# Reciprocal roots of four layer norms on GpSimd, projection biases as weight rows, residual copies by DMA

## The chip, the cores and the metric

One core of one Trainium2 chip runs the whole program. The metric is the device time of one execution in microseconds (us). Engines are named as in the profile: PE (TensorE matmul), PEld (its weight loads), DVE (VectorE), ACT (ScalarE), POOL (GpSimd), SP (SyncE, which here issues transfers).

## The reference, cut to what matters

Sixteen images with their texts give 324 tokens of 192 channels each. Two transformer layers follow. The change touches the first layer (L0) and the shared-key attention of the second (L1), above all the layer norms, the two projection biases and the residual sums.

```python
def _layernorm(x, axis=-1, eps=1e-05):
    m = jnp.mean(x, axis=axis, keepdims=True)
    v = jnp.var(x, axis=axis, keepdims=True)
    return (x - m) / jnp.sqrt(v + eps)
...
h = _L0_tok_ref(x, L0_tok_W)
h = jnp.concatenate([h, txt], axis=1)
h = h + _L0_attn_ref(_layernorm(h), ..., L0_attn_W_proj, L0_attn_b_proj)      # ends in  out @ W_proj + b_proj
h = h + _L0_ffn_ref(_layernorm(h), ...)
h = h + _L1_attn_ref(_layernorm(h), ..., L1_attn_W_proj, L1_attn_b_proj)      # softmax attention, out @ W_proj + b_proj
h = h + _L1_ffn_ref(_layernorm(h), ...)                                       # a second norm of its own, router, attention, MLP
```

## The kernel before

Tokens lie on partitions: 324 tokens are three tiles of 108 partitions (P = 108, T = 3), 192 channels in the free dimension. The program has two stages. The first goes through the 16 batches and does everything up to the spill of the routed inputs; the second stage does the last feed-forward block. Between them two passes weave both.

A pass of the first stage works on several batches at once. The string ORDER_1 lists its steps, and every engine walks the same list in the same order, doing its own share of each step. OFF_1 says by how many batches a step runs ahead. In the string `s` is one score matmul with its exponential, `a` the weighted sum of values, `m` one block of scores whose row maximum DVE takes (`mxh`), `r` the transposes that bring the maxima (`mp`) to rows. The named steps are those of the layers: `ln1` to `ln4` the norms, `t1` to `t5` transposes of normed tokens, `tok` the patch embedding, `qk`, `v`, `val`, `hid`, `out`, `proj`, `proj4` products. Each engine works strictly in this order, so a step that waits holds back every step behind it on its engine.

Each norm is cut in steps: step 0 takes statistics (`bn_stats`, tile `st`), step 1 aggregates them to mean and variance (tile `mv`) and starts a Newton iteration for the reciprocal root (a first guess from the bits in tile `rs`, then three rounds of three small DVE instructions, tile `nt`), step 2 does two of the rounds, step 3 subtracts the mean and multiplies (`normalised`, tiles `xn`, for ln4 `xna` and `xn5`). For ln4 the root of a second norm directly behind it comes out of the same variances. Each of these small instructions waits for the one before it (`link`). Ring buffers in PSUM (`lin` with two banks for products, `mps` with three for the maxima) tie DVE and ACT to PE: PE may fill a bank only when its reader has emptied it.

The residual sums read an addend from SBUF: `hb` is the token tile plus the bias of the first projection, `hab` is `hc` plus the bias of the second, and `hc` is a copy of `h` from one pass to the next. POOL makes all three (steps `hb`, `hab`, `hc`), besides bf16 pieces of q and k (`parts`, tile `piece`) and `hx`. POOL also issues the fetch of the next tokens (`xload`). SP issues the other transfers in the order of the list: the pieces to DRAM (`todram`, scr_q and scr_k), from there packed into `qpack` and `kpack` (`pack0` to `pack2`), the softmax denominators out and their reciprocals back (`den`, `spread`, tile `bc`).

Of the kernel before, what the change touches and what calls it, by code (L numbers as in the profile page):

```python
# [30 lines left out]
EPS4, EPS5 = 1e-5, 1e-6  # L31
# [231 lines left out]
def build(nc, A):  # L263
# [3 lines left out]
    with ctx:  # L267
# [16 lines left out]
        b_p0 = sb("b_p0", [P, C])  # L284
# [5 lines left out]
        b_p1 = sb("b_p1", [P, C])  # L290
# [19 lines left out]
        hb = sb("hb", [P, T, C])  # L310
# [5 lines left out]
        mv = sb("mv", [P, T, 2])  # L316
        var = sb("var", [P, 2 * T])
        rs = sb("rs", [P, 2 * T])
        nt = sb("nt", [P, 2 * T])
# [195 lines left out]
        ln4_done = signal("ln4_done", 2)  # L515
        nmz_ready = signal("nmz_ready")
# [24 lines left out]
        MEMSETS_POOL, SETUP_POOL, SETUP_DVE = 10, 14, 10  # L541
# [9 lines left out]
        NFIRST, NLOAD = len(FIRST) + 1, len(LOADS) + 7  # L551
# [8 lines left out]
        def _(sp):  # L560
# [4 lines left out]
            sp.dma_start(b_p0[:, :], A["b_p0"].partition_broadcast(P)).then_inc(loads_first.sem, 16)  # L565
# [9 lines left out]
            sp.dma_start(b_p1[:, :], A["b_p1"].partition_broadcast(P)).then_inc(loads.sem, 16)  # L575
# [45 lines left out]
            def denominators(att, name, k, j):  # L621
# [13 lines left out]
                else:  # L635
# [79 lines left out]
        def _(pool):  # L715
# [6 lines left out]
            for n, (x, value) in enumerate(((of[64:KP, :, :, :], 0.0), (xS[KC:KP, :, :], 0.0), (v1[:, :, :, :], 0.0),  # L722
# [3 lines left out]
                                            (bc[:, :, :], 1.0))):  # L726
# [35 lines left out]

            def first_step(name, k, c, what, j, i):
                if name == "shared":
                    shared_pieces()
                    both_layers()
                elif name == "xload":
# [3 lines left out]
                    pool.wait_ge(hb_ready.sem, hb_ready.at(j - 1, 1))  # L771
# [6 lines left out]
                elif name == "hab":  # L778

                    front.emptied(pool, i, "proj4_1")  # L780
                    pool.wait_ge(hc_ready.sem, hc_ready.at(j, 1))
                    for t in range(T):
                        done = nc.gpsimd.tensor_tensor(hab[:, t, :], hc[:, t, :], b_p1[:, :], ALU.add)
                    done.then_inc(hab_ready.sem, 1)
                elif name == "hc":

                    front.emptied(pool, i, "out_1")
                    pool.wait_ge(hab_ready.sem, hab_ready.at(j - 1, 1))
                    pool.sem_inc(gate_pool.sem)
                    nc.gpsimd.tensor_copy(hc[:, :, :], h[:, :, :]).then_inc(hc_ready.sem, 1)  # L790
                elif name == "hb":

# [842 lines left out]
```

## Time and profile before

| | |
|---|---|
| median of 3 runs | 2161.02 us (2160.82 to 2162.99) |
| the profiled execution's own time | 2163.17 us |
| its span, first to last instruction | 2161.4 us |
| PE busy | 1898.0 us, 88% |
| DVE busy | 1425.0 us, 66% |
| ACT busy | 1119.6 us, 52% |
| POOL busy | 267.0 us, 12% |
| mean granted TensorE clock | 0.962 |

The rows further down come from the profiled execution, so their sums are held against 2161.4 us of span. A row of a timeline has the start in us, the length, engine, line, operation and tiles, how many instructions it merges, and in brackets how long the engine was idle before it and for whom. One pass of the first stage takes about 82 us. PE busy time counts a matmul until its modelled end, so PE counts as idle only when nothing at all is under way on it.

### The profile page before, as it was taken

What the parts mean: (1) busy time and instruction counts of PE and PEld (TensorE: products, weight loads), DVE (VectorE), ACT (ScalarE), POOL (GpSimd) and SP (SyncE); (2) the same over time, 40 slices, a digit from 0 to 9 for tenths busy, and PEclk for the clock granted to TensorE, in tenths of its full rate; (3) what the DMA queues carried; (4) which work ended last, traced back from release to release, by engine and by line L of the source; (5) the groups of instructions that cost most, each with busy time, mean ns of one, the idle gap of its engine ahead of it and who ended that gap; (6) DMA issues with size and microseconds to landing.
All of it is one profiled execution on the core that took longest, in us unless ns stands there. A gap on an engine that the chain in (4) does not pass through costs nothing. (4 is left out here: it accounts for less than half of the span.)

```text
span 2161.4 us, 42850 instructions
## 1 busy us (share of the span) xinstructions
PE 1898.0 (88%) x11904; PEld 1267.3 (59%) x11904; DVE 1425.0 (66%) x4566; ACT 1119.6 (52%) x2585; POOL 267.0 (12%) x406
## 2 busy tenths in 40 slices
PE   3688998998998998998998987767899999999996
PEld 2465665666665666665665654434566666666664
DVE  3267777767867867868868866524677656566563
ACT  1244554554554554554554554353565656566563
POOL 4301101101101101101101101100011001001000
PEclk9799999999999999999999999978999999999998
DMA  4202112112112112112122021302334333433431
GB/s 150 53 16 55 49 32 61 37 39 60 42 39 56 40 45 57 40 47 57 37 51 57 27 55 51 80 25 68 76 89 114 78 97 94 110 93 89 115 83 35
DMA packets 157452, 134.86 MB, mean 62 GB/s; under 512 B 31924, under 2 KB 136344, under 8 KB 157208
## 3 DMA queue, kind: packets, MB, share of 16 engines
q1 hardware_dynamic: 153592, 127.90, 22.7%
q0 software_dynamic: 2304, 4.79, 0.9%
q8 instruction: 58, 0.95, 0.2%
q10 hardware_dynamic: 1440, 0.75, 0.1%
q14 instruction: 58, 0.48, 0.1%
HBM read 81.96 MB, written 50.16 MB: 61 GB/s over the span
## 5 line engine op out<-in xcount | busy, mean ns | idle before, releaser
L1228 DVE TENSOR_REDUCE mxh<-mps 108x1 f32<-108x260 f32 (+1 forms) x1728 | 684.5, 442 | 351.2 <-PE mps L1400 340.3
L943 ACT ACTIVATE prob<-sps 108x324 f32<-108x324 f32 x1536 | 623.1, 439 | 523.5 <-PE sps L1370 477.6
L1400 PE MATMUL mps<-kpack,qpack 96*108 96x260 bf16 (+1 forms) x1728 | 420.9, 298 | 56.2 <-DMA kpack<-scr_k 25.0
L1370 PE MATMUL sps<-qpack,kpack 128*108 128x324 bf16 x1536 | 440.8, 321 | 33.4 <-ACT prob L943 26.7
L1400 PEld LDWEIGHTS mps<-kpack,qpack 96*108 96x108 bf16 x1728 | 220.5, 131 | 210.4 <-DVE mxh L1228 86.7
L1385 PE MATMUL aps<-prob,v 128*32 128x324 f32 x3072 | 318.5, 459 | 3.7 <-ACT prob L943 1.2
L1370 PEld LDWEIGHTS sps<-qpack,kpack 128*108 128x108 bf16 x1536 | 192.2, 129 | 211.8 <-ACT prob L943 149.9
L1356 PE MATMUL lin<-yT,w 128*128 128x324 f32 x576 | 186.0, 455 | 18.1 <-ACT g L843 13.7
L1356 PEld LDWEIGHTS lin<-yT,w 128*128 128x128 f32 x576 | 103.6, 194 | 63.8 <-issue 32.7
L1385 PEld LDWEIGHTS aps<-prob,v 128*32 128x32 f32 x3072 | 73.2, 110 | 105.2 <-issue 60.3
L758 POOL CAST piece<-rest 128x324 bf16<-128x324 f32 x96 | 43.6, 454 | 729.5 <-DVE rest L1060 721.9
L777 POOL TENSOR_TENSOR hx<-ha,xna 108x576 f32<-108x576 f32 x16 | 22.4, 1397 | 863.2 <-DVE xna L1030 863.2
L1356 PE MATMUL lin<-xT,w_in 128*128 128x324 f32 x384 | 119.8, 445 | 0.5 <-ACT xT L839 0.5
L1346 PE MATMUL lin<-w,g 128*108 128x192 f32 x576 | 108.0, 329 | 2.7 <-PEq L136 2.7
L1346 PE MATMUL lin<-w_out,g 128*108 128x192 f32 x576 | 108.1, 330 | 2.0 <-PEq L136 2.0
L1329 PE MATMUL lin<-ident,xn 108*96 108x108 f32 x384 | 62.2, 284 | 46.3 <-DVE xn L1030 37.5
L957 ACT COPY av<-aps 128x324 f32<-128x324 f32 x96 | 41.1, 428 | 103.2 <-PE aps L1385 78.0
L1346 PEld LDWEIGHTS lin<-w,g 128*108 128x108 f32 x576 | 91.2, 173 | 5.7 <-issue 3.4
L1346 PEld LDWEIGHTS lin<-w_out,g 128*108 128x108 f32 x576 | 92.0, 176 | 4.2 <-issue 2.5
L943 ACT ACT_TABLE_LOAD x65 | 83.4, 1283 | 14.8 <-PE sps L1370 12.9
L843 ACT ACT_TABLE_LOAD x66 | 84.7, 1283 | 8.7 <-PE lin L1356 7.6
L1356 PEld LDWEIGHTS lin<-xT,w_in 128*128 128x128 f32 x384 | 68.0, 193 | 28.2 <-ACT g L843 5.1
(157 smaller groups left out, 2402.4 us busy)
## 6 DMA issues: line engine op xcount, KB each, us to landing
qpack<-scr_q SPq DMA_DIRECT2D x96, 243.0 KB, 3.3
kpack<-scr_k SPq DMA_DIRECT2D x96, 121.5 KB, 3.3
scr_q<-piece SPq DMA_DIRECT2D x32, 243.0 KB, 3.1
scr_k<-piece SPq DMA_DIRECT2D x32, 243.0 KB, 4.0
kpack<-scr_k SPq DMA_DIRECT2D x96, 81.0 KB, 3.1
bc<-rec_d SPq DMA_DIRECT2D x128, 60.8 KB, 2.4
scr_q<-piece SPq DMA_DIRECT2D x32, 162.0 KB, 3.5
scr_q<-piece SPq DMA_DIRECT2D x64, 81.0 KB, 3.4
```

Source lines behind the costliest of these rows:

```text
L758: nc.gpsimd.tensor_copy(piece[:, m, 1, :], rest[:, m, :]).then_inc(att.second.sem, 1)
L777: nc.gpsimd.tensor_tensor(hx[:, :, :], ha[:, :, :], xna[:, :, :], ALU.add).then_inc(hx_ready.sem, 1)
L843: nc.scalar.activation(g[:, f, :], ring.at(i, what)[:, 0:N], ACT.Gelu, bias=b_in[:, f:f + 1] if bias else 0.0).then_inc(ring.free["act"].s ...
L943: nc.scalar.activation(prob[0:rows, n % NP, :], sps[0:rows, n % 2, 0:N], ACT.Exp, scale=SCALE).then_inc(att.exped.sem, 1)
L957: nc.scalar.copy(av[:, q, :], aps[:, 0:N]).then_inc(att.copied.sem, 1)
L1228: nc.vector.tensor_reduce(mxh[:, hd, t, s:s + 1], att.mps.at(i, use)[0:P, 0:att.width], AX.X, ALU.max, negate=True).then_inc(att.mps.free[ ...
L1329: done = nc.tensor.transpose(b[0:KC, t * P:(t + 1) * P], src[:, t, k * KC:(k + 1) * KC], ident[0:P, 0:P])
L1346: done = mm(tiles2(b)[0:P, t % 2, :], acts[k][:, t * P:(t + 1) * P], weights[k], start=k == 0, stop=k == 5)
L1356: done = mm(b[0:size, 0:N], w[:, k, c:c + size], x[:, k, 0:N], start=k == 0, stop=k == 1)
L1370: mm(sps[0:rows, n % 2, 0:N], kpack[:, 4 * q + n % 4, k * att.rows:k * att.rows + rows], qpack[:, 4 * q + n % 4, :], start=True, stop=True ...
L1385: mm(aps[32 * hd:32 * hd + 32, 0:N], att.values[:, k, 4 * q + hd, :], prob[:, n % NP, :], start=k == 0, stop=k == kt - 1).then_inc(att.sum ...
L1400: mm(bank[0:P, 0:att.width], qpack[0:6 * D, 4 * q + hd, t * P:(t + 1) * P], kpack[0:6 * D, 4 * q + hd, s * att.width:(s + 1) * att.width], ...
```

## The change

Four things are changed.

- The Newton iterations leave DVE. DVE's step 1 of a norm is now only the aggregation (into `mean`, one tile for each norm), which signals POOL. POOL adds the epsilon (`vars4`; for ln4 a second instruction makes the variance of the second norm) and raises the result to the power -0.5 with one `tensor_tensor`, operation pow, against a tile of -0.5. DVE's step 3 (for ln4 its step 2 and 3) waits for POOL's `root`. Step 2 of ln1 to ln3 is gone, and `hx` is listed behind ln4_2.
- Both projection biases become a row of the weights. For the first, row 96 of `aT` is set to one and row 96 of `w_p0` holds the bias. For the second the softmax denominator row of head 0 is multiplied by its own reciprocal and so is one; for this one of the four `bc` transfers writes 32 partitions where it wrote 16. The matmuls keep their number and shape.
- `hc` and `hab` become transfers that SP issues, 108x576 each. `hb` is gone: the residual of `proj` reads the token tile `hin` itself.
- The next tokens are fetched behind `proj_1`, at the end of a pass; it stood behind `dft_0.0`, some three slots of the list earlier.

```diff
 ORDER_1 = (
-    "a ln2_1 m m m s v_0.0 s ln2_2 ln2_3 s s m v_0.1 m s m p v_1.0 s recip s",
+    "a ln2_1 m m m s v_0.0 s ln2_3 s s m v_0.1 m s m p v_1.0 s recip s",
...
-    "hid5 m m s s m proj4_0.0 m den m proj4_0.1 s spread0 spread1 proj4_1 s s ln4_0 a s hx ln4_1 r ln4_2 s",
+    "hid5 m m s s m proj4_0.0 m den m proj4_0.1 s spread0 spread1 proj4_1 s s ln4_0 a s ln4_1 r ln4_2 hx s",
...
-    "s m s ln3_0 tok.0 s tok.1 m m m s hab t4_0 t4_1 ln3_1 s m hb m a m log m s t5_0",
-    "exp p m ln3_2 s s ln3_3 t5_1 s m m s a",
+    "s m s ln3_0 tok.0 s tok.1 m m m s hab t4_0 t4_1 ln3_1 s m m a m log m s t5_0",
+    "exp p m s s ln3_3 t5_1 s m m s a",
...
-    "a s t1_0 t1_1 s s ln1_2 ln1_3 zv s",
-    "val_0.0 zs val_0.1 s val_1 pack0 zt s m m m dft_0.0 m m xload p pack1 m a m s m m dft_0.1 m s m m dft_1.0 m m",
+    "a s t1_0 t1_1 s s ln1_3 zv s",
+    "val_0.0 zs val_0.1 s val_1 pack0 zt s m m m dft_0.0 m m p pack1 m a m s m m dft_0.1 m s m m dft_1.0 m m",
...
-    "inv_0.1 inv_1.0 inv_1.1 s r proj_0.0 proj_0.1 proj_1 s ln2_0 a",
+    "inv_0.1 inv_1.0 inv_1.1 s r proj_0.0 proj_0.1 proj_1 xload s ln2_0 a",
...
                     for hd in range(4):
-                        sp.dma_start(bc[32 * hd:32 * hd + D, :, :], rec_d[hd].partition_broadcast(D)).then_inc(att.bc_in.sem, 16)
+                        n = 32 if hd == 0 and att is one else D
+                        sp.dma_start(bc[32 * hd:32 * hd + n, :, :], rec_d[hd].partition_broadcast(n)).then_inc(att.bc_in.sem, 16)
...
+                elif name == "hc":
...
+                    sp.dma_start(hc[:, :, :], h[:, :, :]).then_inc(hc_ready.sem, 16)
+                elif name == "hab":
...
+                    sp.dma_start(hab[:, :, :], hc[:, :, :]).then_inc(hab_ready.sem, 16)
...
+            def reciprocal_roots(n, j):
+
+                pool.wait_ge(spread_known[n].sem, spread_known[n].at(j, 1))
+                pool.sem_inc(gate_pool.sem)
+                nc.gpsimd.tensor_scalar(vars4[:, n, 0], mean[n][:, :, 1], EPS4, None, ALU.add).then_inc(vars_known[n].sem, 1)
+                if n == 3:
+                    nc.gpsimd.tensor_scalar(vars4[:, n, 1], mean[n][:, :, 1], 1.0 + EPS5, EPS4 * EPS5, ALU.mult,
+                                            ALU.add).then_inc(vars_known[n].sem, 1)
+                w = 2 if n == 3 else 1
+                pool.wait_ge(vars_known[n].sem, vars_known[n].at(j, w))
+                nc.gpsimd.tensor_tensor(root[n][:, 0:w, :], vars4[:, n, 0:w, :], minus_half[:, 0:w, :],
+                                        ALU.pow).then_inc(root_known[n].sem, 1)
...
                     pool.wait_ge(ln1_done.sem, ln1_done.at(j - 1, 1))
-                    pool.wait_ge(hb_ready.sem, hb_ready.at(j - 1, 1))
+                    front.emptied(pool, i, "proj_1")
...
-            def newton(w, times):
-                for _ in range(times):
-                    link(nc.vector.tensor_tensor(nt[:, 0:w], rs[:, 0:w], rs[:, 0:w], ALU.mult))
-                    link(nc.vector.scalar_tensor_tensor(nt[:, 0:w], nt[:, 0:w], -0.5, var[:, 0:w], ALU.mult, ALU.mult))
-                    link(nc.vector.scalar_tensor_tensor(rs[:, 0:w], nt[:, 0:w], 1.5, rs[:, 0:w], ALU.add, ALU.mult))
-
-            def variances(w):
+            def variances(n):
                 for t in range(T):
...
+                    done = nc.vector.bn_aggr(mean[n][:, t, :], st[:, t, :])
+                done.then_inc(spread_known[n].sem, 1)
...
                 else:
-                    normalised(src, dst, rs).then_inc(signals.sem, 1)
+                    dve.wait_ge(root_known[n].sem, root_known[n].at(j, 1))
+                    normalised(src, dst, n, root[n][:, 0]).then_inc(signals.sem, 1)
...
-                    residual(front, i, what, k, h, hb)
+                    residual(front, i, what, k, h, hin)
...
-        "w_p0": padded(rows(a["L0_attn_W_proj"], KC)),
-        "b_p0": a["L0_attn_b_proj"],
+        "w_p0": with_bias(padded(rows(a["L0_attn_W_proj"], KC)), a["L0_attn_b_proj"], KC, 1),
...
-        "w_p1": by_heads(a["L1_attn_W_proj"]),
-        "b_p1": a["L1_attn_b_proj"],
+        "w_p1": with_bias(by_heads(a["L1_attn_W_proj"]), a["L1_attn_b_proj"], D, 0),
```

The first place is DVE around the second norm: the aggregation (`mv` before, `mean` after), the root, three row maxima (`mxh`), and the normalisation `xn`. Before:

```order
L1017 BN_AGGR mv<-st 108x2 x3
L1019 TENSOR_SCALAR var<-mv 108x3
L1025 TENSOR_SCALAR rs<-var 108x3
L1011 TENSOR_TENSOR nt<-rs 108x3
L1012 SCALAR_TENSOR_TENSOR nt<-nt,var 108x3
L1013 SCALAR_TENSOR_TENSOR rs<-nt,rs 108x3
L1228 TENSOR_REDUCE mxh<-mps 108x1 x3
```

Six more Newton instructions follow there before the normalisation. After the change:

```order
L1034 TENSOR_TENSOR h<-lin,hin 108x384
L1034 TENSOR_TENSOR h<-lin,hin 108x192
L1007 BN_STATS st<-h 108x6 x3
L1003 ISA
L1012 BN_AGGR mean<-st 108x2 x3
L1209 TENSOR_REDUCE mxh<-mps 108x1 x3
L1017 TENSOR_SCALAR xn<-h,mean,root 108x192 x3
```

Between the aggregation and the normalisation only the three maxima are left, and the normalisation waits for POOL's `root`.

The second place is POOL over one pass, from `hx` to the fetch of tokens. Before:

```order
L777 TENSOR_TENSOR hx<-ha,xna 108x576
L783 TENSOR_TENSOR hab<-hc,b_p 108x192 x3
L800 TENSOR_TENSOR hb<-hin,b_p 108x192 x3
L790 COPY hc<-h 108x576
L758 CAST piece<-rest 128x324
L760 TENSOR_TENSOR piece<-rest,piece 128x324
```

After the change, from the fetch of one pass to the first piece of the next:

```order
L725 DMA pT<-in_x 128x392
L726 DMA hin<-in_txt 20x192
L727 DMA hin<-in_txt 108x192
L776 TENSOR_SCALAR vars<-mean 108x3
L782 TENSOR_TENSOR root<-vars,minus_half 108x3
L776 TENSOR_SCALAR vars<-mean 108x3
L778 TENSOR_SCALAR vars<-mean 108x3
L782 TENSOR_TENSOR root<-vars,minus_half 108x6
L802 TENSOR_TENSOR hx<-ha,xna 108x576
L776 TENSOR_SCALAR vars<-mean 108x3
L782 TENSOR_TENSOR root<-vars,minus_half 108x3
L767 CAST piece<-rest 128x324
```

The three issues of the fetch now stand directly ahead of the root of ln2; the wide root is that of ln4, and the last root that of ln3. The root of ln1 comes behind the three pairs of pieces.

## Rows read from the trace of the kernel before

**Rows 1.** First line of the page.

```profile
span 2161.4 us, 42850 instructions
```

**Rows 2.** Windows: us, then busy time of each engine, clock, DMA.

```profile
120.00:1306.00 1186.00, 1073.20 (x6994) 731.28 (x6995) 885.83 (x3059) 624.63 (x1477) 150.05 (x238) 0.98 0.17 45
```

**Rows 3.** Waits of PE from 120 to 1306: total, times, longest.

```profile
PE lin L1329 <- DVE xn L1030: 20.1, 34, 1.1
...
PE mps L1400 <- DMA kpack<-scr_k: 14.8, 13, 1.8
...
PE mps L1400 <- DVE mxh L1228: 10.1, 20, 1.5
```

**Rows 4.** Waits of PE from 1306 to 1480, the woven passes.

```profile
PE mps L1400 <- DVE mxh L1228: 5.0, 4, 2.1
...
PE lin L1337 <- DVE ha L1049: 1.9, 2, 1.5
```

**Rows 5.** Waits of PE from 0 to 120, the start.

```profile
PE lin L1329 <- DVE xn L1030: 16.7, 3, 6.0
```

**Rows 6.** Groups by line on DVE: busy us, mean ns, idle before.

```profile
L1011 DVE TENSOR_TENSOR nt<-rs 108x3 f32<-108x3 f32 (+1 forms) x192 | 43.7, 228 | 6.5 <-DVEq L140 1.7
```

**Rows 7.** Groups by line on POOL.

```profile
L800 POOL TENSOR_TENSOR hb<-hin,b_p 108x192 f32<-108x192 f32 x48 | 27.0, 588 | 67.0 <-issue 30.3 <-ACT hin L882 29.8 <-ACTq L140 6.8
L777 POOL TENSOR_TENSOR hx<-ha,xna 108x576 f32<-108x576 f32 x16 | 22.4, 1397 | 863.2 <-DVE xna L1030 863.2
...
L1625 POOL MEMSET const-float32-1.0<- 128x1 f32 x1 | 0.1, 108 | 0.0
```

**Rows 8.** Timeline of DVE around ln2 of one pass.

```profile
701.36 1.01 DVE L1049 TENSOR_TENSOR h<-lin,hb 108x384 f32<-108x384 f32 x2 [1.72 <-PE lin L1337]
...
703.83 0.31 DVE L1017 BATCH_NORM_AGGREGATE mv<-st 108x2 f32<-108x6 f32 x3 [0.55 <-DVE st L1006]
...
707.47 0.96 DVE L1030 TENSOR_SCALAR xn<-h,mv,rs 108x192 f32<-108x192 f32 x3
```

**Rows 9.** Timeline of PE, its first transposes for ln2.

```profile
708.56 0.48 PE L1329 MATMUL lin<-ident,xn 108*96 108x108 f32 x3 [0.51 <-DVE xn L1030]
```

**Rows 10.** Timeline of DVE around ln3, same pass.

```profile
656.35 0.30 DVE L1017 BATCH_NORM_AGGREGATE mv<-st 108x2 f32<-108x6 f32 x3
...
657.47 0.56 DVE L1011 TENSOR_TENSOR nt<-rs 108x3 f32<-108x3 f32 x1
...
662.21 0.96 DVE L1030 TENSOR_SCALAR xn<-h,mv,rs 108x192 f32<-108x192 f32 x3
```

**Rows 11.** Timeline of DVE around ln1, same pass.

```profile
671.68 0.30 DVE L1017 BATCH_NORM_AGGREGATE mv<-st 108x2 f32<-108x6 f32 x3
...
675.48 0.96 DVE L1030 TENSOR_SCALAR xn<-hin,mv,rs 108x192 f32<-108x192 f32 x3
```

**Rows 12.** Timeline of POOL beside it.

```profile
671.95 0.45 POOL L758 CAST piece<-rest 128x324 bf16<-128x324 f32 x1 [1.22 <-DVE rest L1060]
672.49 0.80 POOL L760 TENSOR_TENSOR piece<-rest,piece 128x324 bf16<-128x324 f32 x1
677.22 0.58 POOL L717 DMA_DIRECT2D pT<-in_x  x1 [3.93 <-PE lin L1329]
```

**Rows 13.** Timeline of PE, its transposes for ln1.

```profile
676.57 0.76 PE L1329 MATMUL lin<-ident,xn 108*96 108x108 f32 x6 [0.75 <-DVE xn L1030]
```

**Rows 14.** Timeline of DVE around ln4, same pass.

```profile
726.89 0.31 DVE L1017 BATCH_NORM_AGGREGATE mv<-st 108x2 f32<-108x6 f32 x3
...
729.53 0.96 DVE L1030 TENSOR_SCALAR xna<-ha,mv,rs 108x192 f32<-108x192 f32 x3
```

**Rows 15.** Waits of SP's queue over one pass, 650 to 732.

```profile
SPq L614 <- ACT prob L943: 20.4, 2, 20.2
```

**Rows 16.** Timeline of SP: issue of the bc transfers.

```profile
711.23 1.69 SPq L641 DMA_DIRECT2D bc<-rec_d  x4
```

**Rows 17.** Timeline of DVE: the multiplication that reads bc.

```profile
719.48 1.16 DVE L1075 TENSOR_TENSOR av<-av,bc 128x972 f32<-128x972 f32 x1
```

More of the change, by code:

```diff
@@ L315, in build @@
         st = sb("st", [P, T, 6])
[L316 to L319, printed above, removed]
+        mean = [sb(f"mean{n}", [P, T, 2]) for n in range(4)]
+        root = [sb(f"root{n}", [P, 2, T]) for n in range(4)]
+        vars4 = sb("vars4", [P, 4, 2, T])
+        minus_half = sb("minus_half", [P, 2, T])
         xT1 = sb("xT1", [KP, 2, N])
@@ L508, in build @@
         x_in = signal("x_in", 48, prime=0)
-        hb_ready = signal("hb_ready")
-        hab_ready = signal("hab_ready")
-        hc_ready = signal("hc_ready")
+        hab_ready = signal("hab_ready", 16)
+        hc_ready = signal("hc_ready", 16)
         ln1_done = signal("ln1_done")
@@ L515, in build @@
         ln4_done = signal("ln4_done", 2)
+        spread_known = [signal(f"ln{n + 1}_spread") for n in range(4)]
+        root_known = [signal(f"ln{n + 1}_root") for n in range(4)]
+        vars_known = [signal(f"ln{n + 1}_vars", 2 if n == 3 else 1) for n in range(4)]
         nmz_ready = signal("nmz_ready")
@@ L721, in _ @@
             load_x(0)
-            for n, (x, value) in enumerate(((of[64:KP, :, :, :], 0.0), (xS[KC:KP, :, :], 0.0), (v1[:, :, :, :], 0.0),
+            for n, (x, value) in enumerate(((of[64:KP, :, :, :], 0.0), (aT[KC:KP, :, :], 0.0), (aT[KC:KC + 1, :, :], 1.0),
+                                            (xS[KC:KP, :, :], 0.0), (v1[:, :, :, :], 0.0),
                                             (kpack[KC:KP, :, :], 0.0), (yA[KC:KP, :, :], 0.0),
@@ L766, in first_step @@
                     both_layers()
+                elif name in ("ln1", "ln2", "ln3", "ln4"):
+                    if k == 1:
+                        reciprocal_roots(number(name) - 1, j)
                 elif name == "xload":
@@ L777, in first_step @@
                     nc.gpsimd.tensor_tensor(hx[:, :, :], ha[:, :, :], xna[:, :, :], ALU.add).then_inc(hx_ready.sem, 1)
[L778 to L791, printed above, removed]
-                    if isinstance(i, int) and i == -2:
-                        pool.wait_ge(loads_first.sem, 16 * NFIRST)
-                    else:
-                        front.emptied(pool, i - 1, "proj_1")
-                    front.emptied(pool, i, "tok")
-                    pool.wait_ge(x_in.sem, x_in.at(j, 48))
-                    for t in range(T):
-                        done = nc.gpsimd.tensor_tensor(hb[:, t, :], hin[:, t, :], b_p0[:, :], ALU.add)
-                    done.then_inc(hb_ready.sem, 1)
                 elif name == "qk":
@@ L976, in _ @@
         def _(dve):
-            for x in (xT1[KC:KP, :, :], aT[KC:KP, :, :], vz[KC:KP, :, :], xT2[KC:KP, :, :], qpack[KC:KP, :, :], cntb[:, :, :],
+            for x in (xT1[KC:KP, :, :], vz[KC:KP, :, :], xT2[KC:KP, :, :], qpack[KC:KP, :, :], cntb[:, :, :],
                       selall[:, :], gateall[:, :], work[:, :]):
@@ L1176, in first_step @@
                     elif k == 1:
[L1177 to L1178 removed]
+                        variances(3)
                     elif k == 2:
[L1180 to L1187 removed]
+                        dve.wait_ge(root_known[3].sem, root_known[3].at(j, 1))
+                        normalised(ha, xna, 3, root[3][:, 0]).then_inc(ln4_done.sem, 1)
+                    else:
+                        dve.wait_ge(root_known[3].sem, root_known[3].at(j, 1))
+                        normalised(ha, xn5, 3, root[3][:, 1]).then_inc(ln4_done.sem, 1)
                 elif name == "log":
@@ L1578, in by_heads, with with_bias @@
         return w.reshape(GROUPS, 128, C).transpose(1, 0, 2)
+    def with_bias(w, b, p, k):
+        w = w.copy()
+        w[p, k] = b
+        return w
     nh = a["x"].shape[2] // 16
```

57 lines of the change are left out of this document (18 added, 39 removed), and 2 rows, old and new, of the table OFF_1.

## The prediction

> **What bounds the kernel now.** I read the windows by stage first, then PE's waits in the same windows, then DVE, POOL, PE and SP in the timeline of one pass. The span is 2161.4 us [rows 1]. In the passes of the first stage PE is busy for 1073.2 of 1186 us, DVE for 885.8 [rows 2]: PE is the bound, with 9.5% of the time in which nothing is under way on it. So work taken off DVE is worth only what PE's idle time before it was worth. In that window PE waited 20.1 us for normed tokens, 10.1 us for a bank of maxima that DVE had not yet read, and 14.8 us for the transfer that fills `kpack` [rows 3]. In the woven passes it waited 5.0 us for the maxima and 1.9 us for a residual sum [rows 4], at the start three times for normed tokens, 16.7 us in all [rows 5]. The reader should see that the named DVE waits which the norms can cause are some 35 us in all after the start, and that the second stage has no norm in it.
>
> **The Newton instructions.** Each norm has eleven of them (epsilon, first guess, nine of three rounds), ln4 fifteen: 48 for a batch, 768 in all. A group of them has a mean of 228 ns [rows 6], so they take about 10 us of DVE in a pass of 82. What that is worth is read norm by norm; take P as the time of one power on POOL.
>
> **The new chain.** Aggregation, hand-over to POOL, addition, power, hand-over to DVE. A hand-over costs 0.13 us: `xn` ends at 707.47 + 0.96 = 708.43 [rows 8] and PE starts at 708.56 [rows 9]. From one POOL instruction to the next that waits for it are 672.49 - (671.95 + 0.45) = 0.09 us [rows 12]. POOL's additions take 588 ns for 192 elements and 1397 ns for 576, so 2.1 ns an element and 0.19 us at three elements; a memset of one element takes 108 ns [rows 7]. The chain is T = 0.13 + 0.19 + 0.09 + P + 0.13 = P + 0.54, and P + 0.73 for ln4 with its second addition.
>
> P has no row. Below it is bounded by an addition, 0.19 us. Above I take a power as a logarithm, a product and an exponential, some 25 steps; if each cost as much as a whole small instruction, that is 25 x 0.19 = 4.8 us. The work is three elements a partition in one instruction, without 25 dispatches, so it is nearer the lower end: I take 1 us, T = 1.54, and keep 0.2 and 4.8 for the range. The Trainium skill, page "GPSIMD Engine Reference", section "Engine selection", says to keep elementwise work on VectorE and that GPSIMD is about twice as slow with two inputs. If that held against the whole Newton string of ln4, the power would cost 4.6 us and the kernel would be slower; no row here shows a power.
>
> **ln2.** The aggregation ends at 704.14, the normalisation starts at 707.47: 3.33 us [rows 8], and PE then waited 0.51 [rows 9]. With three maxima still between, T up to 3.33 - 0.51 = 2.82 removes the whole wait, so P up to 2.3.
>
> **ln3.** From 656.65 to 662.21 are 5.56 us [rows 10]: POOL has room for any P here. Five Newton instructions stood ahead of the maxima, one of them 0.56 us long beside POOL's `hb`, and PE waited for the maxima behind them; `hb`, `hab` and `hc` leave POOL too. The 10.1 us of waits for maxima should go.
>
> **ln1.** POOL is busy with a piece until 673.29 [rows 12], so the root starts there, and `xn` at 673.29 + 1.54 = 674.83 where it was at 675.48 [rows 11]. PE's wait of 0.75 [rows 13] shrinks by 0.65. But this gives nothing in the end: the `kpack` transfer behind it depends on pieces made before ln1 and not on the norm, and PE already waited 14.8 / 13 = 1.1 us for it in a pass [rows 3]. What PE gains ahead, it waits there. The same cover protects: T up to 675.48 - 673.29 + 1.1 = 3.3 us costs nothing.
>
> **ln4.** DVE has no work between aggregation and normalisation, 727.20 to 729.53, 2.33 us [rows 14]. New: 1.73. P above 1.6 makes everything behind it late, one for one.
>
> **The sum.** Normed tokens: 20.1 us less the share of ln1, 14 passes x 0.75 = 10.5, leaves 9.6. Maxima: 10.1. Woven passes: the Newton strings are part of why DVE is late there; I take half of 5.0 + 1.9, 3.4. Start: four norms are waited for openly, and each chain gets shorter by about 2.33 - 1.54 = 0.8, so 3 us. Together 26 us. 2161.4 - 26.1 = 2135.3 us of span; the profiled execution had 1.8 us around its span (2163.17) and stood 2.15 above the median, so 2135 as a median.
>
> **What I cost at nothing.** `hc` and `hab` as transfers: SP issues two more in a pass, some 0.35 us each, and stands 20.4 us in one wait for ACT [rows 15]; they read and write long before their users a pass or half a pass later. Behind `hc` on SP stands the store of pieces; without cover it would be late by 0.35 a pass, 5 us in all. The wider `bc` transfer: issued until 712.92 [rows 16], read at 719.48 [rows 17], 6.5 us of cover. Bias rows: same matmuls; two memsets more on POOL at the start, where its first root may be 0.5 us late. The fetch at the end of the pass has half a pass until `tok`. But its three issues of about 0.58 us [rows 12] now run from 702.4, when the last `h` is summed [rows 8], to about 704.15, and the root of ln2 stands behind them; its aggregation ends at 704.14, so they cost nothing.
>
> **The rivals.**
> *The power is slow, so the kernel is slower.* The place is DVE's new wait in ln4, where nothing else can run, with row maxima queued behind it for which PE waits. It decides from the point at which ln4's loss (P - 1.6) eats the gains of 0.51 at ln2 and about 1 at ln3: at P = 2.7, ln2 keeps 0.1, ln4 loses 1.1. At P = 4 a pass has T = 4.54: ln2 +1.2, ln3 -1.0, ln1 +1.2, ln4 +2.4, so +3.8; 14 passes and 5 us at the start make +58, 2219 us. For it: a power in software has no row, and the string it replaces took only 2.33 us. Against: three elements. Chance 0.15.
> *The fetch delays ln2.* POOL's issues were made while DVE stood idle; now they run beside its statistics. If they took three times as long, 5.2 us, the root would be known at 709.2, 2.2 us past the room; 14 times 2.2 less the 26 gained, and 7 lost at ln2's share: about 2173. Nothing in the rows shows such a stretch. Chance 0.05.
> *The gain is given back.* PE leaves each gap earlier only to find ACT's exponentials or transfers not ready, as at ln1. Then only start and woven passes give anything, 6 us: 2155 to 2160. Chance 0.13, of which 0.08 lies within 0.2%.
> *DVE's lead is worth more than the named waits.* Busy PE hides short stalls in its modelled ends; 10 us less DVE work a pass could shorten those and the 10.5 us of ln1 too: up to 50 us, 2111. Chance 0.12.
> *The forecast*, 2122 to 2150, holds 0.55.
>
> **How the numbers follow.** 2135 is the likeliest case. The range 2108 to 2180 takes in the given-back gain, the stronger gain and the delayed fetch, and leaves out most of the slow power. 0.2% is 4.3 us, about what a measurement of this kernel can tell from no change. Faster by more: 0.55 + 0.12 + 0.05 = 0.72. Same: 0.08. Slower: 0.15 + 0.05 = 0.20.
>
> **What would show it.** In the trace after, POOL's power on 108x3 should be near 1 us, and DVE in ln4 should stand idle for about 1.7 us between aggregation and `xna`. PE's waits for normed tokens in the passes should fall from 20.1 to under 10 us and the wait for maxima to near zero, while that for `kpack` stays or grows by about what ln1 gave. A pass should be 1.4 us shorter. A power over 2.7 us, POOL issues stretched beyond a microsecond, or a `kpack` wait that grows by more than ln1's share would make it wrong.

## The result and the profile after

The kernel after took 2093.71 us (median of 4 runs, 2092.38 to 2097.8), before 2162.01 us (4 runs): ratio 0.9687, 95% interval 0.967 to 0.9704, 68 us faster. The same kernel on two other chips (e9 and e16 below) stood at 0.972 (0.9703 to 0.9738) and 0.9718 (0.97 to 0.9736) of before, 61 us faster. Forecast were a gain of 26 us and a time of 2135 us, with a range from 2108 to 2180. The direction was right, and the size was less than half of what came.

The page after and its groups on POOL (busy, mean ns of one, idle before):

```profile
span 2090.6 us, 42205 instructions
...
PE 1876.9 (90%) x11904; PEld 1262.7 (60%) x11904; DVE 1271.1 (61%) x3797; ACT 1112.2 (53%) x2583; POOL 289.0 (14%) x441
...
L782 POOL TENSOR_TENSOR root<-vars,minus_half 108x3 f32<-108x3 f32 (+1 forms) x64 | 63.9, 999 | 5.3
L776 POOL TENSOR_SCALAR vars<-mean 108x3 f32<-108x3 f32 x64 | 15.4, 241 | 564.3 <-DVE mean L1012 563.6 <-POOL minus_half L738 0.3
```

The price with no row is known now: the power takes 0.88 us on 108x3 and 1.35 us on 108x6, 1.0 in the mean of all (taken: 1 for each), the addition 0.24 (taken: 0.19). DVE lost 154 us of busy time. PE's busy time fell by 21 us too (1898.0 before), though it runs the same 11904 matmuls. That is the first sign of where the rest of the gain lies.

PE's waits after, in the passes (110 to 1242), answer to [rows 3]:

```profile
PE sps L1351 <- ACT prob L944: 22.1, 60, 1.1
...
PE mps L1381 <- DMA kpack<-scr_k: 6.5, 9, 1.0
...
PE mps L1381 <- DVE mxh L1209: 1.4, 6, 0.3
PE lin L1310 <- DVE xn L1017: 0.7, 1, 0.7
```

Normed tokens (20.1) and maxima (10.1) are gone from the list, as forecast, and more fully than forecast, which left up to 10 us for the tokens. The wait for `kpack`, which was to stay, fell from 14.8 to 6.5 in this execution; two later ones of the same kernel have 15.6 and 13.1. The woven passes (1242 to 1413) answer to [rows 4]: nearly nothing changed.

```profile
PE mps L1381 <- DVE mxh L1209: 4.1, 5, 1.6
...
PE lin L1318 <- DVE ha L1034: 2.0, 2, 1.5
```

DVE's new waits in the passes, the first at ln1 and ln2 (at ln3 the root is ready in time), the second at ln4:

```profile
DVE xn L1017 <- POOL root L782: 40.4, 29, 2.5
DVE xna L1017 <- POOL root L782: 30.4, 14, 2.2
```

At ln4 it is 2.17 us a pass, 0.44 more than the 1.73 forecast; 0.35 of it is POOL's power on 108x6, which takes 1.35 us and not 1.

**Where the time came from.** The kernel has sixteen `hx` instructions, one a pass. From the first to the fourteenth are thirteen passes: 81.9 us each before, 77.6 after, 78.2 in e9. The start up to the first `hx` went from 238.3 to 227.3 us (e9: 228.0). From the sixteenth to the end e9 took as long as before, 691.6 us; the first execution took 687.2. Windows of those thirteen passes, before and then e9 (us, busy time of PE, PEld, DVE, ACT, POOL with their instructions, clock, DMA):

```profile
238.30:1302.80 1064.50, 964.79 (x6332) 657.10 (x6331) 805.39 (x2788) 563.08 (x1339) 137.67 (x219) 0.98 0.18 47
```

```profile
228.00:1245.20 1017.20, 940.15 (x6332) 651.29 (x6331) 678.54 (x2164) 557.01 (x1340) 154.12 (x244) 0.99 0.21 56
```

The same 6332 matmuls: the stretch is 47.3 us shorter, PE's idle time fell from 99.7 to 77.1 (by 22.7) and its busy time by 24.6. Half of the gain was never visible as idle time. The granted clock (0.98 and 0.99) does not explain it, since forms of matmul that nobody kept waiting have the same mean. What got shorter are the transposes, which stood behind the stalls (by 4.9 us in all), the matmuls of the maxima (by 3.6) and those of the scores (by 3.3). Groups of PE in these windows, before and then e9:

```profile
L1356 PE MATMUL lin<-xT,w_in 128*128 128x324 f32 x312 | 96.3, 440 | 0.0
L1346 PE MATMUL lin<-w_out,g 128*108 128x192 f32 x469 | 87.3, 326 | 0.0
...
L1329 PE MATMUL lin<-ident,xn 108*96 108x108 f32 x312 | 49.2, 277 | 19.1 <-DVE xn L1030 18.9
```

```profile
L1337 PE MATMUL lin<-xT,w_in 128*128 128x324 f32 x312 | 96.2, 439 | 0.0
L1327 PE MATMUL lin<-w_out,g 128*108 128x192 f32 x469 | 87.3, 325 | 0.0
...
L1310 PE MATMUL lin<-ident,xn 108*96 108x108 f32 x312 | 44.3, 257 | 0.0
```

### The profile page after: what moved, and what is told of

Read it like the earlier page. It is cut to its first block and busy times, and to the rows that moved or that the text cites. A ratio compares the mean times of both kernels' runs of the same rounds, so it can differ in the third digit from the quotient of the medians.

```text
span 2090.6 us, 42205 instructions
## 1 busy us (share of the span) xinstructions
PE 1876.9 (90%) x11904; PEld 1262.7 (60%) x11904; DVE 1271.1 (61%) x3797; ACT 1112.2 (53%) x2583; POOL 289.0 (14%) x441
## 5 line engine op out<-in xcount | busy, mean ns | idle before, releaser
L1381 PE MATMUL mps<-kpack,qpack 96*108 96x260 bf16 (+1 forms) x1728 | 416.0, 296 | 34.3 <-DMA kpack<-scr_k 14.4
L776 POOL TENSOR_SCALAR vars<-mean 108x3 f32<-108x3 f32 x64 | 15.4, 241 | 564.3 <-DVE mean L1012 563.6
L944 ACT ACT_TABLE_LOAD x64 | 82.1, 1283 | 14.8 <-PE sps L1351 13.0
L1045 DVE TENSOR_TENSOR rest<-lin,piece 128x324 f32<-128x324 f32 x96 | 47.2, 492 | 61.9 <-ACT piece L854 28.3
```

The source lines that it names most:

```text
L776: nc.gpsimd.tensor_scalar(vars4[:, n, 0], mean[n][:, :, 1], EPS4, None, ALU.add).then_inc(vars_known[n].sem, 1)
L944: nc.scalar.activation(prob[0:rows, n % NP, :], sps[0:rows, n % 2, 0:N], ACT.Exp, scale=SCALE).then_inc(att.exped.sem, 1)
L1045: nc.vector.tensor_tensor(rest[:, m, :], ring.at(i, what)[:, 0:N], piece[:, m, 0, :], ALU.subtract).then_inc(ring.free["dve"].sem, 1)
L1381: mm(bank[0:P, 0:att.width], qpack[0:6 * D, 4 * q + hd, t * P:(t + 1) * P], kpack[0:6 * D, 4 * q + hd, s * att.width:(s + 1) * att.width], ...
```

## The experiments

Seventeen runs. "Against before" is the ratio with its interval of 95%, "pass" the mean of the thirteen passes in the profiled run in us. The last three columns are PE's waits from 130 to 1230 us: for normed tokens (`xn`), for maxima (`mxh`) and for `kpack`.

| run | against before | pass | xn | mxh | kpack |
|---|---|---|---|---|---|
| before | 1 | 81.9 | 18.1 | 9.5 | 14.1 |
| after | 0.9687 (0.967 to 0.9704) | 77.6 | 0.7 | 1.1 | 6.5 |
| e1 Newton strings back | 0.9827 (0.9804 to 0.985) | 79.8 | 19.2 | 2.0 | 5.3 |
| e2 roots only | 0.9765 (0.9734 to 0.9795) | 78.7 | none | 1.1 | 17.3 |
| e3 fetch late only | 0.9966 (0.9949 to 0.9982) | 81.5 | 11.9 | 10.1 | 2.5 |
| e4 after, fetch early | 0.9769 (0.9744 to 0.9794) | 79.0 | none | 0.8 | 24.8 |
| e5 copies and rows only | 0.9894 (0.9875 to 0.9913) | 80.8 | 19.4 | 1.7 | 14.6 |
| e6 power twice | 0.9819 (0.9793 to 0.9844) | 79.9 | 11.1 | 10.4 | 9.9 |
| e7 copies on POOL | 0.9738 (0.9717 to 0.976) | 78.4 | 0.8 | 0.4 | 9.6 |
| e8 last piece on DVE | 0.9746 (0.9724 to 0.9767) | 78.6 | 0.7 | 0.7 | 17.7 |
| e9 after again | 0.972 (0.9703 to 0.9738) | 78.2 | 0.7 | 0.8 | 15.6 |
| e10 power twice in ln4 | 0.979 (0.9774 to 0.9806) | 79.1 | 0.7 | 10.3 | 12.5 |
| e11 maximum in ln4 | 0.9715 (0.9698 to 0.9731) | 78.0 | 0.7 | 1.1 | 13.0 |
| e12 scores in inv | 0.9749 (0.9735 to 0.9763) | 78.2 | 0.7 | 1.1 | 15.3 |
| e13 store by ACT | 0.9711 (0.9696 to 0.9725) | 77.9 | 0.7 | 1.1 | none |
| e14 e13 and e8 | 0.9713 (0.97 to 0.9727) | 78.1 | 0.7 | 1.1 | 0.2 |
| e15 e13 and e11 | 0.9679 (0.9666 to 0.9692) | 77.9 | 0.7 | 1.1 | none |
| e16 after, third time | 0.9718 (0.97 to 0.9736) | 78.0 | 0.7 | 1.1 | 13.1 |
| e17 e15, beside e16 | 0.969 (0.9674 to 0.9705) | 78.1 | 0.7 | 1.1 | 0.9 |

**e1 to e4: one part undone, or one part alone.** The theory after the first comparison was that the Newton strings were the loss and stalls longer than they look; the rivals were the transfers and POOL's copies.

e1 takes the kernel after and puts the Newton code back:

```diff
+                    newton(T, 2)
...
-                    dve.wait_ge(root_known[n].sem, root_known[n].at(j, 1))
-                    normalised(src, dst, n, root[n][:, 0]).then_inc(signals.sem, 1)
+                    normalised(src, dst, rs).then_inc(signals.sem, 1)
```

> The kernel after, with the Newton strings back on DVE in their old places; the two transfers for the residual copies, the bias rows and the late fetch stay. Theory S (the strings were the loss: each stall of PE behind them was 0.25 to 0.35 us longer than its visible idle time, and this holds at ln1 too): nearly all of the 68 us comes back, 2145 to 2160 us. Theory T (transfers: the late fetch shortens the chain from the pieces to kpack, which is what let the gain at ln1 through): about a third of the gain stays, 2130 to 2145. Theory C (hb, hc and hab left POOL, which sped up DVE beside them): half or more stays, 2120 to 2135.

Measured: 0.9827, 1.07% above e9, 23 us; its 2129 us lie inside Theory C's range. Theory S, which wanted nearly all of the gain back, falls; 37 us of the gain stay without the roots.

e2 is before with `reciprocal_roots` on POOL, with the steps of the list that this changes, and nothing else:

> The kernel before, with only the roots moved to POOL; hb, hc and hab stay POOL's, the biases are added as before, the fetch stays early. Theory S: 2093 to 2108 us, within 15 us of the kernel after. Theory T: ln1's share of some 1.1 us a pass is waited for at kpack again, so 2108 to 2125. Theory C: POOL's copies stand in the way of the roots (a root behind hb or hc waits up to 1.5 us) and slow DVE, 2120 or more. If the parts simply add, this kernel and e1 lie as far from before and after as each other.

Measured: 0.9765, 51 us faster than before. Theory C's obstacle did not show, and PE's wait for normed tokens is gone with a wait for `kpack` of 17.3. What the roots give alone (51) and what remains without them (37) add up to more than the whole: two parts remove the same loss. Where it lies comes with e5.

e3 is before with this alone:

```diff
-    "... dft_0.0 m m xload p pack1 ...
+    "... dft_0.0 m m p pack1 ...
...
-    "inv_0.1 inv_1.0 inv_1.1 s r proj_0.0 proj_0.1 proj_1 s ln2_0 a",
+    "inv_0.1 inv_1.0 inv_1.1 s r proj_0.0 proj_0.1 proj_1 xload s ln2_0 a",
...
+                    front.emptied(pool, i, "proj_1")
                     pool.sem_inc(gate_pool.sem)
```

> The kernel before, with only the fetch of the next tokens moved behind the projection. Theory T: the issue of qpack, which stood behind the stores of pieces, comes some 0.5 us earlier in a pass, PE's wait for kpack falls from 14.8 us to about 8, and the time by 5 to 10 us (2151 to 2157). Theory S: DVE's ln1 is what PE waits for first, so less than 4 us either way (2158 to 2166). If POOL's three issues cost something beside ln2's statistics, it is slower by up to 14 x 0.5 = 7 us.

Measured: 0.9966, 7 us, with the wait for `kpack` down from 14.1 to 2.5 us.

e4 is after with `xload` back behind `dft_0.0` and a step `hb` by which SP copies the tokens, `sp.dma_start(hb[:, :, :], hin[:, :, :])`, since `hin` is overwritten early:

> The kernel after, with the fetch early again, for which the tokens are copied to hb by a transfer in every pass. Theory T: the fetch runs beside the stores of pieces again, kpack comes 0.5 us or more later in each pass and PE waits for it: 7 to 15 us slower than after, 2100 to 2108. Theory S: less than 4 us slower, 2090 to 2098.

Measured: 0.9769; against e9 10.6 us slower, with 24.8 us of waits for `kpack` where e9 has 15.6. It has the added copy in it, so not all of this need be the fetch. Both runs agree with Theory T in sign and size. The medians from issue to landing of the packs, in before and in e3:

```profile
qpack<-scr_q SPq DMA_DIRECT2D x39, 243.0 KB, 3.4
kpack<-scr_k SPq DMA_DIRECT2D x39, 121.5 KB, 3.9
```

```profile
qpack<-scr_q SPq DMA_DIRECT2D x39, 243.0 KB, 3.1
kpack<-scr_k SPq DMA_DIRECT2D x39, 121.5 KB, 3.3
```

In e4 these medians are 3.2 and 3.3 although the fetch is early, so they alone do not carry the reading. The starts in the timelines do: from the issue of a pass's first pack to PE's first matmul on the new `kpack` it took 5.1 us in e4 and 4.6 in e9, means of the thirteen passes.

**e5: the copies and bias rows alone.** e1 with e4's fetch, so Newton on DVE and the fetch early (`hx` is listed behind ln4_2, as in after):

> The kernel before, with hb, hc and hab made by transfers and the biases as weight rows; Newton strings on DVE and the fetch early. e1 and e3 differ in just these copies and stand 1.4% apart. Theory C (POOL's additions slow DVE's Newton instructions beside them: the first guess 259 ns in before, 172 in e1; nt 231 and 200): the strings are as slow or fast whatever the fetch does, so a similar 20 to 30 us, ratio to before 0.986 to 0.991. Theory K (what DVE gains is waited for at kpack as long as the fetch runs ahead of the packs, as in e2 and e4): under 12 us, ratio 0.994 or more, and PE's wait for kpack at 20 us or more.

Measured: 0.9894, 23 us faster, inside Theory C's range. The waits for maxima are gone (1.7 us) with every Newton instruction still there. The timeline of DVE at ln3 shows why. In e5:

```profile
645.43 0.17 DVE L1011 TENSOR_SCALAR var<-mv 108x3 f32<-108x3 f32 x1
645.63 0.17 DVE L1017 TENSOR_SCALAR rs<-var 108x3 int32<-108x3 int32 x1
645.84 0.16 DVE L1003 TENSOR_TENSOR nt<-rs 108x3 f32<-108x3 f32 x1
```

and in before, where POOL makes `hb` from 655.72 to 657.41 and `hc` behind it:

```profile
656.92 0.51 DVE L1025 TENSOR_SCALAR rs<-var 108x3 int32<-108x3 int32 x1
657.47 0.56 DVE L1011 TENSOR_TENSOR nt<-rs 108x3 f32<-108x3 f32 x1
658.06 0.16 DVE L1012 SCALAR_TENSOR_TENSOR nt<-nt,var 108x3 f32<-108x3 f32 x1
...
655.72 1.69 POOL L800 TENSOR_TENSOR hb<-hin,b_p 108x192 f32<-108x192 f32 x3 [3.73 <-ACT hin L882]
657.35 0.66 POOL L790 COPY hc<-h 108x576 f32<-108x576 f32 x1
```

Beside a POOL instruction two of the string took 0.51 and 0.56 us in place of 0.17 and 0.16. Each ended 0.02 us behind POOL's instruction beside it: at 657.43 behind the last addition of `hb` (657.41), at 658.03 behind the copy `hc` (658.01). The Trainium skill, page "Advanced Engine Details and Errata", section "Mode Summary" under "VectorE Performance Modes", says that VectorE's second SBUF port is shared with GpSimd and that GpSimd's instructions and VectorE's two-port ones block each other; the rows agree with a block, though they do not show which port it is. At the end of ln4 the same happens beside `hab`. In before:

```profile
732.10 0.51 DVE L1185 TENSOR_TENSOR nt<-nt,rs 108x3 f32<-108x3 f32 x1
732.65 0.52 DVE L1186 TENSOR_TENSOR nt<-nt,rs 108x3 f32<-108x3 f32 x1
...
732.01 1.68 POOL L783 TENSOR_TENSOR hab<-hc,b_p 108x192 f32<-108x192 f32 x3
```

and in e5:

```profile
720.66 0.16 DVE L1177 TENSOR_TENSOR nt<-nt,rs 108x3 f32<-108x3 f32 x1
720.86 0.16 DVE L1178 TENSOR_TENSOR nt<-nt,rs 108x3 f32<-108x3 f32 x1
```

Over the thirteen passes the small instructions and the second normalisation at these two places are 22 us shorter in e5. This loss goes when the strings leave or when the copies leave. That is the overlap: roots alone 2.35%, copies and rows alone 1.06%, both (e4) 2.31% and not 3.41%, which makes 24 us. It lies in one stretch, and both places lie in it. From `hx` to the last piece of q and k a pass took 24.5 us before, 23.2 in e5, 22.6 in e2 and 22.7 in e4: 1.3 and 1.9 alone but 1.8 together, so 1.4 us a pass and 22 us in sixteen are counted twice.

**e7: after with `hc` and `hab` on POOL.**

```diff
-                    sp.dma_start(hab[:, :, :], hc[:, :, :]).then_inc(hab_ready.sem, 16)
+                    nc.gpsimd.tensor_copy(hab[:, :, :], hc[:, :, :]).then_inc(hab_ready.sem, 1)
```

> The kernel after, with hc and hab as copies by POOL again (no bias in them; each some 0.66 us or more for 576 elements), no transfers. Theory C1 (POOL's copies cost only through the Newton strings, which are gone): within 5 us of after, ratio to before 0.966 to 0.971. Theory C2 (they slow whatever DVE does beside them): 5 to 15 us slower than after, 0.971 or more.

Measured: 0.9738, by its own figures Theory C2's case, but those were set against the first 0.9687. Against e9 (0.972) the difference of 0.18% lies within the intervals: with the strings gone the copies cost 4 us or nothing, as Theory C1 has it.

**e6 and e10: the length of the power.** In e6 every norm computes it twice, in e10 only ln4:

```diff
+                nc.gpsimd.tensor_tensor(spare[:, 0:w, :], vars4[:, n, 0:w, :], minus_half[:, 0:w, :], ALU.pow)
                 nc.gpsimd.tensor_tensor(root[n][:, 0:w, :], vars4[:, n, 0:w, :], minus_half[:, 0:w, :],
```

> The kernel after, with each power computed twice (the first one's result is not used), so the chain of a norm is longer by 0.88 us, that of ln4 by about 1.35. By the prediction's steps: ln2 and ln3 have room, ln1 is covered at kpack, and ln4 counts one for one beyond what it took before: 16 x 1.35 = up to 22 us slower. By the trace after, in which nothing behind ln4 came earlier than before though DVE was 1.3 us earlier there: DVE has room behind ln4 too, so under 8 us slower, and what there is comes from ln1 and the start (2.5 us).

> The kernel after, with the second power only in ln4 (1.35 us more there). By the prediction's step (DVE has nothing else to do there, maxima are queued behind, so everything behind it is late one for one): 16 x 1.35, some 20 us slower than after. By the trace of e6, in which the pass was 2.4 us longer and 0.85 of it lay at ln1 and 0.54 at ln2: about 1.1 a pass, 12 to 18 us slower. If the maxima have room: under 5 us.

Measured against e9: e6 21 us slower, e10 15. Ln4's 1.35 us more are 0.9 us a pass; not quite one for one, and the wait is where the prediction put it, at the maxima queued behind:

```profile
PE mps L1384 <- DVE mxh L1212: 10.3, 18, 0.7
```

The slack that I had read out of the trace after is not there. The other three norms together cost some 6 us for 0.85 us more each. The intervals of e6 and e10 overlap, but PE's wait for normed tokens is 11.1 us in e6 and 0.7 in e10. The prediction had these norms free up to a power of 2.3 us, and two powers are 1.73. At ln2 the room had gone to the fetch: its three issues stand ahead of the root, and POOL's addition starts 0.7 to 1.1 us behind DVE's aggregation, and 0.2 at the other norms. In one pass of e6 the aggregation ends at 604.38 and the normalisation starts at 607.23, 2.85 us later, where the prediction had room for 2.82, and PE waits 0.30.

**e9: after again.** It was run because e7 and e8 both came out slower than after.

> The kernel after, unchanged, beside before on the chip of these runs. In its own trace the store of the last pieces landed in a median of 3.2 and 2.7 us, in that of e1, e4, e7 and e8 in 3.7 and 3.3 (before 3.7 and 3.3), and kpack waits for that store. If this belongs to the kernel, it shows 3.2 and 2.7 again and a ratio of 0.967 to 0.970. If it belongs to that one execution or chip, it shows 3.7 and 3.3 here and a ratio near those of e7 and e8, 0.972 to 0.976, and then e4, e6, e7 and e8 have to be read against this run.

Measured: the stores land in 3.7 and 3.2 us (3.2 and 2.7 in the first trace), and the ratio is 0.972. So 0.3% of the first result belonged to that chip or execution, and a wait for `kpack` of this size belongs to the kernel (13.1 us in e16, with landings of 3.4 and 2.9):

```profile
scr_k<-piece SPq DMA_DIRECT2D x14, 243.0 KB, 3.7
...
scr_k<-piece SPq DMA_DIRECT2D x14, 121.5 KB, 3.2
```

```profile
PE mps L1381 <- DMA kpack<-scr_k: 15.6, 13, 1.6
```

**e8, e11, e12: attempts at something faster.** e8 has DVE instead of POOL make the last piece and moves `ln1_1` ahead of `qk2`. e11 puts `ln4_2` and `hx` behind one maximum, e12 moves one score matmul:

```diff
-    "... ln4_0 a s ln4_1 r ln4_2 hx s",
-    "out_0.0 m m out_0.1 ...
+    "... ln4_0 a s ln4_1 r s",
+    "out_0.0 m ln4_2 hx m out_0.1 ...
...
-    "... inv_0.0 s m m p s m s m m s",
-    "inv_0.1 inv_1.0 inv_1.1 s r proj_0.0 ...
+    "... inv_0.0 s m m p s m s m m",
+    "inv_0.1 inv_1.0 inv_1.1 s s r proj_0.0 ...
```

> The kernel after, with the last tile's second and third piece (POOL: 0.45 and 0.80 us) made by DVE right behind its rest, and the aggregation of ln1 ahead of it, so that POOL's root lies beside them. If the chain from the last piece to kpack still sets PE's start (6.5 us of waits in the trace after), it comes 0.3 to 0.6 us earlier a pass: 3 to 8 us faster than after, ratio to before 0.965 or less. If the root of ln1 sets it, its normed tokens come 1.2 us earlier, with the same sign. If DVE's extra 0.8 us a pass is what counts, it is slower by up to 10 us.

> The kernel after, with the normalisation of ln4 (and hx) one maximum later in DVE's order, so that a maximum of 0.42 us lies in DVE's 2.17 us of idle time before it. If DVE's wait in ln4 costs PE one for one, as e10 tests: 0.4 us a pass, 4 to 6 us faster than after. If the kernel after is bound elsewhere there: within 3 us.

> The kernel after, with one matmul of scores moved from between the parts of the inverse transform to where PE waits for aT (0.74 us a pass, 9.5 us in the window of the passes). If that wait is a plain gap that work can fill: up to 0.3 us a pass, 3 to 6 us faster. If PE only waits for aT later or for the exponentials instead: within 3 us, or slower.

Measured: e8 0.9746, e12 0.9749, both some 0.3% above e9 and so misses, e8 with an interval that overlaps e9's; e11 0.9715, no difference. In e12 the wait for `aT` fell only from 9.5 to 8.8 us. SP's timeline of e8, with DVE's line of the last piece, shows why the earlier piece was worth nothing:

```profile
638.18 3.67 SPq L596 DMA_DIRECT2D scr_q<-piece  x6
...
641.14 0.49 DVE L1155 TENSOR_TENSOR piece<-rest,piece 128x324 bf16<-128x324 f32 x1
...
641.89 1.40 SPq L600 DMA_DIRECT2D scr_k<-piece  x2
```

The last piece is ready at 641.63, and SP has only then got through six issues of 0.6 us each.

**e13 to e15 and e17: one store less on SP.** ACT issues the store of the second tile's key piece right behind its own share of `qk2`:

```diff
                 for m, p0, c0, c1 in ((1, 64, 0, 64), (2, 0, 64, C)):
+                    if m == 1 and att is one:
+                        continue
...
+                        act.wait_ge(one.third.sem, one.third.at(j, 2))
+                        act.dma_start(scr_k[:, 0:64, :].rearrange("s p n -> p s n"), piece[64:128, 1, :, :]).then_inc(one.scr_in.sem, 16)
```

> The kernel after, with one of the two stores of key pieces (the one of the second tile, which is ready early) issued by ACT instead of SP. In e8 the last piece was ready at 641.63 but SP issued its stores from 641.89 to 643.29, right behind four to six others. If SP's issues are what the chain to kpack runs through (theory Q), the last store starts some 0.7 us earlier in a pass, PE's wait for kpack falls from 15.6 us (e9) to 7 or less, and the time by 5 to 11 us against e9: ratio to before 0.967 to 0.9695. If the pieces or the landing itself are the bound (theory L), the wait stays at 13 to 17 us and the ratio at 0.971 to 0.974; ACT's issue may cost 2 to 4 us.

> e13 and e8 together: one store by ACT and the last piece by DVE, with ln1's aggregation ahead of it. Theory Q: what e8 could not show behind SP's issues shows now, the last piece is ready 0.6 us earlier and its store starts with it: as fast as e13 or up to 5 us faster. If DVE's added work is what made e8 slower (0.9746 against 0.972), it is slower than e13 by the same 2 to 6 us.

> e13 and e11 together: one store by ACT and a maximum in DVE's idle time in ln4. e11 moved nothing that could be measured (0.9715 against 0.972) while PE still waited 13.0 us for kpack. If that wait took the gain back, it shows here: 2 to 5 us faster than e13. If ln4 at this length of power has nothing to give: the same as e13.

Measured: the wait for `kpack` is gone in all three (0.2 us in e14), so Theory Q names the right resource. But e13 stands at 0.9711 against 0.972: of 15.6 us of wait some 2 came out as time, less than the intervals tell. PE now waits longer for ACT, in e13

```profile
PE sps L1359 <- ACT prob L952: 25.1, 68, 1.1
```

where e9 has 21.4 (58 times). ACT's timeline of e13 shows where that comes from: the store stands ahead of two exponentials and waits for POOL's piece, and they wait with it. In e9 (the last row below) the same two start 0.33 us behind the start of ACT's cast, in e13 2.05.

```profile
639.23 0.43 ACT L856 CAST piece<-lin 128x324 bf16<-128x324 f32 x1 [0.38 <-PE lin L1345]
640.46 0.66 ACTq L919 DMA_DIRECT2D scr_k<-piece  x1
641.28 0.77 ACT L952 ACTIVATE prob<-sps 108x324 f32<-108x324 f32 x2 [1.62 <-POOL piece L771]
```

```profile
638.86 0.43 ACT L854 CAST piece<-lin 128x324 bf16<-128x324 f32 x1 [0.38 <-PE lin L1337]
639.19 0.78 ACT L944 ACTIVATE prob<-sps 108x324 f32<-108x324 f32 x2
```

From the last piece to the first pack's issue a pass takes 3.7 us in e13 and 4.6 in e9, but PE comes to ln1's transposes 26.3 us behind `hx` and not 25.1. The first `hx` came at 231.8, 3.7 us later than in e9, which one profiled execution does not explain. e14 is no better than e13. e15 was the fastest, and its repetition beside the kernel after decides:

> The kernel after, unchanged, as the baseline of e17 on the same chip. Its ratio to before was 0.9687 in its first runs and 0.972 in e9, intervals of 0.0017 either way, so comparisons across chips of less than 0.3% say little; here 0.968 to 0.973.

> The kernel of e15 (one store of key pieces by ACT, one maximum in DVE's idle time in ln4) beside after on the same chip. If it is faster by what e15 and e9 differ: 0.3 to 0.5% below e16, 6 to 11 us, and its start to the first hx and its passes say where. If the difference was that of the chips: within 0.15% of e16.

Measured: e17 0.969 (2095.5 us) beside e16 0.9718 (2101.18 us), 0.28% or 6 us faster, the intervals just overlapping. It is the best version found; that its gain is real is likely, and why e11 and e13 have to go together for it was not shown.

## Why the prediction was too small

**What held.** The power near 1 us, though the 25 steps behind its upper bound of 4.8 rested on no row, so the value was a guess that came out; the chain; the roots free for PE at ln2 and ln3 at that length; maxima and normed tokens gone from PE's waits; the place where a slower power would hurt. The transfers `hc` and `hab` showed no cost, though SP's issues take 0.80 and 0.85 us and not the 0.35 taken; no run tests them or the wide `bc` by themselves. Against the whole string of ln4 the power is not slower: from aggregation to normalisation it takes 2.18 us (694.47 to 696.65 in e9), and the string took 2.33 [rows 14]. The rival of the slow power began at 2.7 us, and no run reached that; with 1.73 (e6) the kernel is still 39 us faster than before.

**The step that failed most** is "work taken off DVE is worth only what PE's idle time before it was worth", and with it every term of the sum taken from [rows 3]. Over thirteen passes the idle time fell by 22.7 us, which scales to 25 for the 1186 us of [rows 2]; the terms for normed tokens and maxima gave 19.7. That part was nearly right, in part by luck: ln1's share, which was left out, came as well, and ACT's exponentials took some back (PE's wait for them from 130 to 1230 us went from 18.2 to 21.4, while that for normed tokens fell by 17.4 and that for maxima by 8.7). The same stretch gave 24.6 us more in which PE counted as busy. At ln2 of one pass PE's visible wait was 0.51 us [rows 9]. From the two score matmuls ahead of it to the transposes it took 0.96 us before and takes 0.30 in e9, which has no wait there: 0.66 us for a visible 0.51. Before and e9 in PE's timelines:

```profile
707.60 0.46 PE L1370 MATMUL sps<-qpack,kpack 128*108 128x324 bf16 x2
708.56 0.48 PE L1329 MATMUL lin<-ident,xn 108*96 108x108 f32 x3 [0.51 <-DVE xn L1030]
```

```profile
675.68 0.46 PE L1351 MATMUL sps<-qpack,kpack 128*108 128x324 bf16 x2
675.98 0.44 PE L1310 MATMUL lin<-ident,xn 108*96 108x108 f32 x3
```

The same comparison of starts at three more stalls of that pass gives 0.92 us for a visible 0.75 (ln1), 0.59 for 0.42 (ln3) and 0.69 for 0.55 (a matmul of maxima at 659.02). So each visible stall hid 0.14 to 0.17 us more, together 0.63 of the 1.40 us by which PE's busy time fell in this pass; for the rest no wait is listed. The section on the profile says that a matmul counts until its modelled end; the prediction used that only for a rival. That rival ("DVE's lead is worth more") named the right mechanism; its bound of 50 us was short of the 61 measured. The fetch and the copies below are not in it.

**"This gives nothing in the end"**, of ln1: its visible 10.5 us were taken out of the sum because `kpack` would take them back. The wait for `kpack` did stay (15.6 us in e9, 14.8 in [rows 3]), yet PE gained 0.9 us a pass at that place. Both are true because the chain to `kpack` became shorter as well. In the mean of the thirteen passes the last piece is ready 1.8 us sooner behind `hx`, the first pack is issued 4.6 us behind it as before, and from there to the matmul that needs `kpack` it takes 4.6 us in e9 and took 5.5 before. Of this 0.9 us e4 leaves 0.5 to the fetch, since with an early fetch it takes 5.1; the rest is not separated.

**The fetch costed at nothing.** At its new place it cost PE nothing, though its issues end 0.7 us behind the aggregation of ln2 and not with it. But its leaving the stretch of the packs had a worth that the prediction never priced: 7 us alone (e3), up to 10.6 with the rest in place (e4). `kpack`'s packs land in 3.9 us in before and in 3.3 in e3. The trace of before has only the first number, but it shows 292 KB of tokens fetched from 677.22 on [rows 12], and the prediction read that as a matter of POOL's time alone.

**The copies costed at nothing** as an edit were worth 23 us by themselves (e5, with the bias rows). [Rows 10] showed the 0.56 us (beside `hc`, not `hb`), and the text named it; it was not asked what a 0.16 us instruction at 0.56 does to all that stands behind it. The mean of 228 ns in [rows 6] was the same sign: it was read as the price of a Newton instruction, and alone one takes 0.16 us.

**Woven passes**, 3.4 us forecast: nothing. The stretch from the fourteenth to the sixteenth `hx` took 167.0 us before, 166.8 after and 166.5 in e9, and the waits of [rows 4] are nearly as they were. Half of them had been guessed to be due to Newton strings; they are not. **Start**: 3 us forecast, 10 up to the first `hx`. At the inverse transforms of the first two batches, some 120 us in, PE was 2.8 to 3.5 us earlier in e9 (4 to 4.6 in the first execution), about the forecast; the rest comes in the passes that follow.

**Left open.** Why two stores land 0.5 us sooner in one execution of the same kernel, worth some 7 us. What the bias rows alone are worth. And where the part of the 24.6 us lies that is not at a visible stall.

## What to carry to other kernels

Where busy time counts until a modelled end, idle time before a wait is a lower bound of what the wait costs. Compare starts: here each of four visible stalls cost 0.14 to 0.17 us more than it showed, and over the passes half of the gain had never been visible as idle time. Before costing a removed copy or a moved fetch at nothing, look at what ran beside it and took longer than its like elsewhere. When two changes together give less than their sum, measure one stretch of the pass in all four versions: the overlap lies where each of them gains alone. A gain that vanishes behind the next wait is worth following to its resource (here SP's queue of six issues), but handing the issue to another engine also hands it the wait that stands before the issue.

## What the runs showed of the hardware

POOL's power on 108x3 elements took 0.88 us and on 108x6 1.35, a second one directly behind it 0.85 and 1.32. DVE instructions of three elements a partition took 0.51 and 0.56 us beside POOL's additions and its copy, ending 0.02 us behind them, and 0.17 and 0.16 without. A transfer of 108x576 f32 issued by SP held its queue for 0.80 and 0.85 us. The same program differed by 0.3% between chips, each time against the kernel before on the same chip.
